# Attention with row scores and maxima four heads ahead, users of two spare banks spread over the batch, features a batch ahead, and two transfers for the shifts

## What is computed

```python
x = L0_attn_x                                    # (32, 256, 128)
xn = _layernorm(x, axis=-1)
x = x + _L0_attn_ref(xn, ...) + _L0_ffn_ref(xn, ...)

# the attention branch, H = 16 heads of D = 8
qc = q - q.mean(axis=-1, keepdims=True)
kc = k - k.mean(axis=-1, keepdims=True)
cov = jnp.einsum('bhsd,bhtd->bhst', qc, kc) / D
q_var = jnp.var(q, axis=-1, ddof=1)
k_var = jnp.var(k, axis=-1, ddof=1)
var_comp = q_var[..., :, None] * k_var[..., None, :] / D
attn = jax.nn.softmax(cov + var_comp, axis=-1)
out = jnp.einsum('bhst,bhtd->bhsd', attn, v)     # then merged and times Wo
```

## Time and profile before

| | before |
|---|---|
| median of 3 runs | 1481.61 us (1475.91 to 1487.62) |
| the profiled execution | 1485.91 us |
| its span in the trace | 1484.1 us |
| TensorE busy | 1282.3 us, 86% |
| VectorE busy | 989.7 us, 67% |
| ScalarE busy | 815.6 us, 55% |
| GpSimd busy | 375.6 us, 25% |

### The profile page before, as it was taken

How to read it: one execution, slowest core, us unless ns; L and a number is a source line. 1 busy time by engine, 2 the same in 40 slices (tenths; PEclk the granted TensorE clock), 3 DMA queues, 4 the chain that set the end, 5 groups by cost and what they waited for, 6 DMA issues and landing times.

```text
span 1484.1 us, 33659 instructions
## 1 busy us (share of the span) xinstructions
PE 1282.3 (86%) x11462; PEld 723.7 (49%) x11462; DVE 989.7 (67%) x2827; ACT 815.6 (55%) x1440; POOL 375.6 (25%) x644
## 2 busy tenths in 40 slices
PE   1788888888888888888887689999999999999998
PEld 1333433343333333333332256666666666666667
DVE  3765555665655556565554478888888888888774
ACT  0245444554545445454545556666676667677744
POOL 5524233342424334242411011111111111111000
PEclk9986566776757767676675689999999999999999
DMA  3000000000000000000000000000000000000000
GB/s 83 5 13 12 13 11 11 11 11 15 8 15 11 11 11 11 15 8 15 12 13 16 25 16 23 23 19 16 14 16 21 21 21 21 21 21 21 15 9 15
DMA packets 50965, 24.91 MB, mean 17 GB/s; under 512 B 6496, under 2 KB 50400, under 8 KB 50912
## 3 DMA queue, kind: packets, MB, share of 16 engines
q1 hardware_dynamic: 50912, 24.21, 6.0%
HBM read 15.28 MB, written 8.39 MB: 16 GB/s over the span
## 4 chain that ended last, share of the span: by engine, by line
PE 57%; ACT 15%; issue 9%; SPq 8%; DVE 6%; DMA 3%; POOL 1%; ACTq 1%; DVEq 0%; POOLq 0%
PE bank L550 51%; SPq L1483 7%; ACT Kexp L1368 6%; ACT hmid L1443 3%; DMA QKT<-shiftT 3%; PE bank L591 3%; DVE smax L1039 2%; ACT shiftT L1353 1%; PE bank L566 1%; ACT prob L1379 1%; PE bank L668 1%; DVE prob L1043 1%; ACT oT L1305 1%; ACT prob L1346 1%; ACT feat L1317 1%
## 5 line engine op out<-in xcount | busy, mean ns | idle before, releaser
L961 DVE TENSOR_REDUCE rowmin<-bank 128x2 f32<-128x512 f32 x512 | 345.8, 689 | 298.9 <-PE bank L550 298.1
L1346 ACT ACTIVATE prob<-bank 128x512 f32<-128x512 f32 x512 | 302.7, 599 | 383.9 <-PE bank L550 382.7
L550 PE MATMUL bank<-QKT 32*128 32x256 f16 x2048 | 252.8, 348 | 49.7 <-DMA QKT<-shiftT 40.0
L550 PEld LDWEIGHTS bank<-w_sb,hmid 128*128 128x128 f32 x2048 | 244.1, 192 | 24.4 <-issue 12.6
L550 PE MATMUL bank<-w_sb,hmid 128*128 128x128 f32 x2048 | 248.5, 276 | 0.5 <-issue 0.5
L1443 ACT ACTIVATE hmid<-bank,up_scale 128x512 f32<-128x512 f32 x256 | 176.2, 733 | 111.4 <-PE bank L550 111.2
L1368 ACT ACTIVATE Kexp<-bank,head_bias,head_mask 128x512 f32<-128x512 f32 x256 | 188.2, 848 | 42.5 <-PE bank L550 42.5
L550 PE MATMUL bank<-prob,V 128*25 128x256 f32 x2048 | 205.0, 535 | 0.0
L1251 DVE SCALAR_TENSOR_TENSOR acc<-bank,gate,acc 128x128 f32<-128x128 f32 x512 | 143.5, 343 | 73.0 <-PE bank L550 71.0
L550 PEld LDWEIGHTS bank<-QKT 32*128 32x128 f16 x2048 | 76.9, 104 | 222.3 <-issue 128.6
L434 POOL TENSOR_TENSOR sq<-feat 128x512 f32<-128x512 f32 x32 | 33.3, 1039 | 444.8 <-ACT feat L1317 227.5
(11 more groups left out here) (177 smaller groups left out, 1683.7 us busy)
## 6 DMA issues: line engine op xcount, KB each, us to landing
QKT<-shiftT SPq DMA_DIRECT2D x512, 1.0 KB
x_in<-in_L_attn_x SPq DMA_DIRECT2D x32, 128.0 KB, 2.1
z_scratch<-z_out SPq DMA_DIRECT2D x32, 128.0 KB, 1.9
xg<-in_L_attn_x SPq DMA_DIRECT2D x64, 64.0 KB, 1.9
zg<-z_scratch SPq DMA_DIRECT2D x64, 64.0 KB, 2.0
out<-acc SPq DMA_DIRECT2D x64, 64.0 KB, 1.6
w_sb<-in_L_ffn_w SPq DMA_DIRECT2D x1, 1024.0 KB, 6.2
wo<-in_L_attn_Wo SPq DMA_DIRECT2D x16, 4.0 KB
```

The lines of the kernel that those rows point to most:

```text
L550: return pe.matmul(o, l, r, start=start, stop=stop, skip_group_check=True)
L961: dve.tensor_reduce(rowmin[h // 8][:, :, h % TILE_ROWS, h // TILE_ROWS % HALF], row_scores[i % 3][:].rearrange("p (s t) -> p s t", s=ST), ...
L1346: act.activation(prob[:, h % 8].rearrange("p t s -> p (t s)"), col_scores[h % 2][:], ACT.Exp, scale=exp_register).then_inc(s_exp, 1)
```

## The change

- The row scores and maxima run four heads ahead of the column scores (`LEAD = 4`, `leading`): in step b, heads 0 to 11 handle row heads 4 to 15 of batch b+1, and heads 12 to 15 row heads 0 to 3 of batch b+2.
- The side work is placed anew in the three tables. On TensorE the order of `misc[1]` is now V (2), half-0 maxima (6), x (9), queries and keys (11), half-1 maxima (14), the last for batch b+1 and no longer for batch b. That of `misc[0]` is half-1 transposes (0), output (3), merge (5), half-0 transposes (8), output projection (11).
- ScalarE copies the features of batch b+3 after head 12 of step b (before: those of batch b+2 after head 0), and GpSimd handles x of batch b+3 and then the features of batch b+3.
- `shift` is laid out with its two parts outermost, so that the rows of one part lie together in `shiftT`, and `place_shift` writes each part with one transfer, whose destination steps over 32 partitions: two transfers for each half instead of eight.
- SyncE's order in a step is load x, place half 0, store the result, place half 1.
- The preparation uses `col_scores[0]` in place of `row_scores[0]`.

```diff
--- before.py
+++ after.py
@@ -29,7 +29,7 @@
 SHIFT = 3 * FEAT
 SPARTS = 2
 SROWS = TILE_ROWS * SPARTS * HALF
-SHIFT_DMAS = TILE_ROWS * SPARTS
+SHIFT_DMAS = SPARTS
 TOP = 2.0 ** 13
 UNIT = 2.0 ** 14
 SLOT = 16
@@ -38,9 +38,10 @@
 
 
 
-PE_AT = dict(half1=1, out=4, merge=6, project=8, half0=12, shift1=1, v=3, shift0=10, x=11, qk=15)
-DVE_AT = dict(half1=2, statistics=0, out=5, shift0=8, half0=13)
-ACT_AT = dict(copy_out=2, features=0, shift1=2, v=4, merged=7, output=9, shift0=11, x=12)
+LEAD = 4
+PE_AT = dict(half1=0, out=3, merge=5, half0=8, project=11, v=2, shift0=6, x=9, qk=11, shift1=14)
+DVE_AT = dict(half1=1, statistics=0, out=4, shift0=5, half0=9, shift1=12)
+ACT_AT = dict(copy_out=2, v=3, merged=6, shift0=7, x=10, features=12, output=13, shift1=15)
 PE_PV = (5, 9, 13, 1)
 
 
@@ -101,6 +102,14 @@
 def row_head(i):
 
     return i ^ 1
+
+
+def leading(b, p, h):
+
+    prev, cur, nxt, prep, norm = present(b)
+    if h + LEAD < H:
+        return nxt, b + 1, 1 - p, h + LEAD
+    return prep, b + 2, p, h + LEAD - H
 
 
 def first_slot(b, h):
@@ -206,7 +215,7 @@
         V = [sb(f"V{p}", [P, ST, VCOLS]) for p in range(2)]
 
         rowmin = [sb(f"rowmin{k}", [P, ST, TILE_ROWS, HALF]) for k in range(2)]
-        shift = [sb(f"shift{k}", [P, ST, TILE_ROWS, SPARTS, HALF], F16) for k in range(2)]
+        shift = [sb(f"shift{k}", [P, ST, SPARTS, TILE_ROWS, HALF], F16) for k in range(2)]
         shiftT = [sb(f"shiftT{k}", [SROWS, NS], F16) for k in range(2)]
         prob = sb("prob", [P, 8, ST, NS])
         oT = sb("oT", [P, 2, NS])
@@ -483,10 +492,9 @@
                 prev, cur, nxt, prep, norm = present(b)
                 own.count = 0
                 pool.sem_clear(s_pool)
-                if prep:
-                    features_stack(b + 2)
                 if norm:
                     normalise_x(b + 3, 1 - p)
+                    features_stack(b + 3)
                 if isinstance(b, int) and NB - 2 <= b < NB:
                     scales(b - (NB - 2))
 
@@ -666,7 +674,7 @@
                 pe.wait_ge(s_shift[k], n + 1)
                 for st in range(ST):
                     ins = pe.transpose(half16(1)[0:SROWS, st * P:(st + 1) * P],
-                                       shift[k][:, st].rearrange("p r j g -> p (r j g)"), identh[:])
+                                       shift[k][:, st].rearrange("p j r g -> p (j r g)"), identh[:])
                 ins.then_inc(s_sht_ps[k], 1)
 
             def hn_transposes(n):
@@ -716,16 +724,20 @@
                 for h in range(H):
                     if cur:
                         col_ready(b, h)
-                    if nxt:
-                        row_ready(b + 1, h)
+                    rows, n, q, i = leading(b, p, h)
+                    if rows:
+                        row_ready(n, i)
                     for half in range(ST):
                         if cur:
                             col_pass(b, p, h, half)
-                        if nxt:
-                            row_pass(b + 1, 1 - p, h, half)
+                        if rows:
+                            row_pass(n, q, i, half)
 
                     if h == PE_AT["half1"] and nxt:
-                        pe.wait_ge(s_half[0], b + 2)
+                        if isinstance(b, int) and b < 2:
+                            pe.wait_ge(s_half[0], b + 2)
+                        else:
+                            pe.wait_ge(s_z, b - 1)
                         stack_transposes(b + 1, 1)
                     if h == PE_AT["out"] and prev:
                         if nxt:
@@ -735,21 +747,17 @@
                         out_transposes(b - 1)
                     if h == PE_AT["merge"] and prev:
                         merge_transposes(b - 1)
-                    if h == PE_AT["project"] and prev:
-                        project_out(b - 1)
                     if h == PE_AT["half0"] and prep:
                         if prev:
-                            pe.wait_ge(s_z, b)
+                            pe.wait_ge(s_oa, b)
                         elif nxt:
                             pe.wait_ge(s_half[1], b + 2)
                         stack_transposes(b + 2, 0)
-
-                    if h == PE_AT["shift1"] and cur:
+                    if h == PE_AT["project"] and prev:
                         if prep:
-                            pe.wait_ge(s_feat, b + 3)
-                        else:
-                            pe.wait_ge(s_sht[0], b + 1)
-                        shift_transposes(b, 1)
+                            pe.wait_ge(s_half[0], b + 3)
+                        project_out(b - 1)
+
                     if h == PE_AT["v"] and nxt:
                         if cur:
                             pe.wait_ge(s_sht[1], b + 1)
@@ -767,6 +775,12 @@
                         xn_transposes(b + 3, 1 - p)
                     if h == PE_AT["qk"] and norm:
                         project_qk(b + 3, 1 - p)
+                    if h == PE_AT["shift1"] and nxt:
+                        if norm:
+                            pe.wait_ge(s_feat, b + 4)
+                        else:
+                            pe.wait_ge(s_sht[0], b + 2)
+                        shift_transposes(b + 1, 1)
                     if h == PE_PV[3] and prev:
                         pv(b - 1, 1 - p, 3)
                     for g in range(3):
@@ -791,8 +805,8 @@
             def prepare():
                 pe.wait_ge(s_zeroed, 1)
                 pe.wait_ge(s_setup, 2)
-                mm(row_scores[0][:, E:E + 1], ones[:], w1_max[:])
-                mm(row_scores[0][:, 0:E], bv_wide[:], out_wT[:]).then_inc(s_bvw, 1)
+                mm(col_scores[0][:, E:E + 1], ones[:], w1_max[:])
+                mm(col_scores[0][:, 0:E], bv_wide[:], out_wT[:]).then_inc(s_bvw, 1)
                 pe.wait_ge(s_setup, 3)
 
             weight_norms()
@@ -966,11 +980,11 @@
                 dve.wait_ge(s_max, H * n + 8 * k + 8)
                 if positive(n):
                     dve.wait_ge(s_sht_ps[k], n)
-                dve.tensor_scalar(shift[k][:, :, :, 0, :], rowmin[k][:], 1.0 / UNIT, None, ALU.mult).then_inc(s_dve, 1)
+                dve.tensor_scalar(shift[k][:, :, 0], rowmin[k][:], 1.0 / UNIT, None, ALU.mult).then_inc(s_dve, 1)
                 dve.wait_ge(s_dve, own.next())
                 for st in range(ST):
-                    ins = dve.scalar_tensor_tensor(out=shift[k][:, st, :, 1, :], in0=rowmin[k][:, st],
-                                                   scalar=1.0 / UNIT, in1=shift[k][:, st, :, 0, :],
+                    ins = dve.scalar_tensor_tensor(out=shift[k][:, st, 1], in0=rowmin[k][:, st],
+                                                   scalar=1.0 / UNIT, in1=shift[k][:, st, 0],
                                                    op0=ALU.mult, op1=ALU.subtract)
                 ins.then_inc(s_shift[k], 1)
 
@@ -1050,8 +1064,9 @@
                 for h in range(H):
                     if h == DVE_AT["half1"] and nxt:
                         half_out(b + 1, 1 - p, 1)
-                    if nxt:
-                        take_max(b + 1, h)
+                    rows, n, q, i = leading(b, p, h)
+                    if rows:
+                        take_max(n, i)
                     if h == DVE_AT["statistics"] and norm:
                         x_statistics(b + 3, 1 - p)
                     if h == DVE_AT["out"] and prev:
@@ -1060,9 +1075,9 @@
                         split_shift(b + 1, 0)
                     if h == DVE_AT["half0"] and prep:
                         half_out(b + 2, p, 0)
+                    if h == DVE_AT["shift1"] and nxt:
+                        split_shift(b + 1, 1)
                     first_head(b, h)
-                if nxt:
-                    split_shift(b + 1, 1)
 
             def first_head(b, h):
                 slot = first_slot(b, h)
@@ -1128,8 +1143,8 @@
                 dve.wait_ge(s_dve, own.next())
                 dve.tensor_tensor(w1_max[:], w1_max[:], w1_scale[:], ALU.max).then_inc(s_setup, 1)
                 dve.wait_ge(s_bvw, 1)
-                dve.tensor_tensor(ob_row[:], row_scores[0][:, 0:E], ob_raw[:], ALU.add)
-                dve.tensor_scalar(w1_sum[:], row_scores[0][:, E:E + 1], 1.0e-30, None, ALU.add).then_inc(s_setup, 1)
+                dve.tensor_tensor(ob_row[:], col_scores[0][:, 0:E], ob_raw[:], ALU.add)
+                dve.tensor_scalar(w1_sum[:], col_scores[0][:, E:E + 1], 1.0e-30, None, ALU.add).then_inc(s_setup, 1)
                 dve.wait_ge(s_setup, 3)
                 dve.tensor_scalar(up_scale[:], w1_sum[:], 1.0 / (HN2_TOP * W1_TOP), None, ALU.mult)
                 dve.reciprocal(w1_scale[:], w1_sum[:]).then_inc(s_dve, 1)
@@ -1385,10 +1400,10 @@
                         probabilities(b, h)
                     if h == ACT_AT["copy_out"] and prev:
                         copy_out(b - 1)
-                    if h == ACT_AT["features"] and prep:
-                        features(b + 2)
-                    if h == ACT_AT["shift1"] and cur:
```

(23 more changed lines are left out.)

## The result

| | before | after |
|---|---|---|
| median of 4 runs | 1484.4 us | 1304.55 us (1300.59 to 1314.88) |
| ratio to before | | 0.8807, 95% interval 0.8742 to 0.8871 |
| span of the profiled execution | 1484.1 us | 1298.3 us |
| TensorE busy | 1282.3 us, 86% | 1127.0 us, 87% |
| VectorE busy | 989.7 us, 67% | 989.6 us, 76% |

The change made the kernel 12% faster. Forecast were 1326 us, within 1245 to 1400; it came out 21 us lower. The kernel does the same work: VectorE's busy time is the same to 0.1 us. TensorE's fell by 155 us with the same 11462 products, so each product got shorter.

What follows compares the result with a forecast made beforehand. It took TensorE's waits and the low clock behind them to bound attention. Steps falling from 23.7 to 18.5 us save 161 us over 31, less 5 at the start: 156 us, hence 1326 us, range 1245 to 1400.

Steps and rivals of the forecast that it cites:

- The waits it named: TensorE in attention: 2.1 us for the maxima transfer, 2.4 before V, 2.0 before x, per two batches; 3.2 us per batch.
- The forecast is wrong if the clock stays near 0.7 or stands at 1.0: Sign for TensorE's mean clock in the attention stage, which was expected at 0.8 to 0.85.
- Two transfers: SyncE's issuing per half falls from 4.8 to 1.2 us; 1.05 us per batch goes, and even eight issues would hide.
- low-clock share: TensorE, each attention step: clock falls once, before x, and about 6 us, 30% of the step, run at the low level.
- wait before x: TensorE before the transposes of x, waiting on GpSimd's 9.3 us chain: about 1 to 2 us at the full level.
- full-clock step: Attention batch at the full clock: 15.5 us, from VectorE's 13.9 us busy plus hand-overs and lumps; 1 us of stall added.
- The lead: Row scores four heads ahead: no work added, moved wait costed at nothing, or up to 0.69 us if cover is gone.
- Full clock throughout: Rival: attention at the full clock all the time, 16 us a step, 234 us saved, 1248 us; chance 0.14.
- GpSimd's chain takes the place of the removed waits: Rival: 9.3 us to x, rest of the step at the low level, 21.8 us, 1428 us; chance 0.07.
- Clock mix unchanged: Rival: only the waits go, attention's clock mix stays; 20 us a step, 110 us saved, 1372 us; chance 0.20.
- slower: Rival: TensorE at the low level throughout attention, 25 us a step, 45 us more, 1527 us; chance 0.05.
- Waits cost twice: TensorE in attention: a wait costs its own length and also low-level work behind it.

Runs made afterwards that it cites:

- a_merge6: The changed kernel with TensorE's merge transposes one head later, at head 6 instead of 5; 1292.8 us, ratio 0.875.
- a_norm_stat10: The changed kernel with GpSimd's normalisation of x one batch earlier and VectorE's statistics at head 10 instead of 14; 1299.0 us, ratio 0.877.
- a_vwait: The changed kernel with the half-1 maxima transposed at head 1 of the next step, so TensorE waits before V again; 1424.7 us, ratio 0.962.
- a_lead0: The changed kernel without the four-head lead, and with the places that depend on it moved back; 1407.7 us, ratio 0.951.
- the fillers: The kernel before with one useless 128-column product ahead of each row score pass, 32 per batch; 1916.8 us, ratio 1.293.
- a_norm_stat10_merge6: The changed kernel with x normalised one batch earlier, statistics at head 10, merge transposes at 6, half-0 maxima at 7; 1278.4 us, ratio 0.864.

## Why the prediction came near, and which of its terms were wrong

- **Direction and size.** The waits it named went away, the clock rose and the time fell. The forecast of 156 us saved stands against 180 measured, 24 us short. That it is so near is in part luck: two wrong terms pulled opposite ways. With the clock up throughout, my own step would have been 15.5 + 1 = 16.5 us and the time 1263 us, 41 us too low. And by its own sign ("The forecast is wrong if the clock stays near 0.7 or stands at 1.0") its account of the clock was wrong: it is 1.00 in 27 of 28 steps.
- **Two transfers.** Right: 1.13 us of issuing, nowhere awaited, and, as the run with eight shows, eight would hide too.
- **The low-clock share was the wrong term.** "The clock falls once, at the wait before x", 30% of the step at the low level. Measured: a mean of 0.98, which is 4% of the window at the low level. That wait is 0.2 us and not 1 to 2, but this alone doesn't explain it: a wait of 1.3 us stands elsewhere in every step, and in a_merge6 waits of 1.06 and 0.71 us, one of them before x, and the clock stays up in both. So the premise that one wait of about 1 us in each step brings the low level was wrong here. As to the wait itself, I had compared GpSimd's 9.3 us with 7.5 us of TensorE's work and left out that TensorE loses 1.3 us in the same stretch, to the output's normalisation, which my sum doesn't have at all, and more in short waits for VectorE. It arrives at x just as x is ready.
- **The full-clock step was the other wrong term, the other way.** I took 15.5 us, VectorE's pace, plus 1 us. It is 17.0, and GpSimd's chain sets it: the wait was small, but the chain was the bound. I had priced it by the wait it shows on TensorE, and a chain that closes over itself shows hardly any. The later merge transposes bear it out: TensorE's wait of 1.3 us removed, the step unchanged, and 0.71 us of waiting before x in its place. TensorE's own order is only 0.1 to 0.2 us shorter (a_norm_stat10), and it takes both edits to get to 16.3 us. VectorE, by which I had set the pace, is busy 363.71 of 450 us, 81%, where I expected 75%, and is not the bound.
- **The sum.** The forecast for the span was 1484.1 - 156 = 1328 us, and it is 1298.3. The step is 17.4 us on average instead of 18.5: 34 us less. The start took 6.6 us (61.50 against 54.90) and the end 1.7, together 8.3 instead of 5: 3 us more. That is the 30 us.
- **The lead.** I costed it at nothing. For the sum that was harmless, since all parts were in it, but as a statement it is not borne out: without it, and with the places that go with it, TensorE waits 1.6 us per batch for maxima, and 103 us are lost.
- **The rivals.** "Full clock throughout" had the clock right and the step (16 us, 1248 us) 1 us too short. "GpSimd's chain takes the place of the removed waits" had the right chain, and a low clock behind it that did not come. "Clock mix unchanged" is refuted. The rule behind it, the clock swinging where products cycle through PSUM banks with short idle times (the Trainium skill, "TensorE: Matmul & The Clock Gate", section on the second failure mode), is not borne out by the kernel after: it cycles through the same three banks, TensorE is busy only 85% (384.64 of 450 us), and the clock is 1.00 in 27 of 28 steps. The kernels with more or longer waits (before, a_vwait, a_lead0) do swing, so the rule holds in some of these kernels and not in others. In the rival "slower", the share with 0.5 us of standing still is 0.10 and not 0.12; the forecast doesn't use it.
- **Waits cost twice.** Shown from both sides: removing 33 us of waits gave 62 us, although another wait came in place of most of them, putting back 43 us (1.4 x 31) cost 120, and filling waits with useless products gave back 65 and 17 us. What exactly makes the clock rise and fall stays open: the fillers of 98% busy time at clock 0.55 show that the busy share in the trace is not it, and a_merge6, with more waiting per step than a_norm_stat10_merge6 and a higher clock, shows that the sum of the waits is not it either.

## What to carry to other kernels

Where TensorE's granted clock stands between its levels, expect that a wait can cost two to three times its length, as two did here, and look first for several waits of 1 us or more close together; but let a run decide, for a_merge6 kept the full clock with 2.4 us of waits per step. If a wait can't be removed, useless products inside it can be cheaper than standing still, but not between 32-row score passes, where they cost 12 us a step. Follow every chain that leads from a step back to itself over other engines, and add it up: it can set the step with waits near zero, and shortening a second way of the same length shows nothing until both are shorter.

## What was new of the hardware

- A wait of 1.40 us followed 3.5 us later by one of 1.30 us brings the low level (probabilities by V 1.91 us instead of 1.06), while the single 1.30 us per step of the kernel after does so once in 28 steps, and 1.06 us followed 2.5 us later by 0.71 us (a_merge6) in none of 28. In a_norm_stat10_merge6, whose longest waits are 0.7 us, ten of 28 steps have the low level.
- A full-size product of 128 columns between 32-row score passes costs far more than itself: 1.30 us for a head with two of them, against 0.53 without, at the low level; and TensorE counts as busy 98% of the time at a clock of 0.55.
- A transfer that steps over 32 partitions with 4 KB takes SyncE 0.53 us to issue, against 0.56 us for one of 1 KB (medians of 128 and of 512).
